# Recommender kernel: a fourth group transposed before the third's products, holds of the gathers moved, layers of the first 256 samples moved into tile 2, last tile in five groups

## What is computed

```python
h = relu(dense @ dw1 + db1)
dense_emb = relu(h @ dw2 + db2)                       # 512 x 64
sparse_emb = emb_tables[f_ids, sparse_idx]            # 512 x 26 x 64
emb = concat([dense_emb[:, None, :], sparse_emb], 1)  # 512 x 27 x 64
inter = einsum('bfd,bgd->bfg', emb, emb)
pairs = inter[:, iu0, iu1]                            # 351 per sample
z = concat([emb.reshape(512, -1), pairs], 1)
z = relu(z @ ow1 + ob1)                               # to 512
z = relu(z @ ow2 + ob2)                               # to 256
z = relu(z @ ow3 + ob3)                               # to 128
return z @ ow4 + ob4
```

## Time and profile before

| | us |
|---|---|
| median of 3 runs | 188.17 (187.83 to 189.74) |
| the profiled execution, its own time | 187.21 |
| its span | 185.4 |
| PE busy / POOL busy in the span | 127.4 / 123.8 |
| DVE busy / ACT busy | 37.8 / 42.2 |

### The profile page before, as it was taken

How to read it: one execution, slowest core, us unless ns; L and a number is a source line. 1 busy time by engine, 2 the same in 40 slices (tenths; PEclk the granted TensorE clock), 3 DMA queues, 4 the chain that set the end, 5 groups by cost and what they waited for, 6 DMA issues and landing times.

```text
span 185.4 us, 3069 instructions
## 1 busy us (share of the span) xinstructions
PE 127.4 (69%) x1301; PEld 68.8 (37%) x1301; DVE 37.8 (20%) x97; ACT 42.2 (23%) x96; POOL 123.8 (67%) x199
## 2 busy tenths in 40 slices
PE   1510285828655995839439993959729979989994
PEld 0000132514344442524226432424426446656453
DVE  2700003000142204100144005000234023136011
ACT  0440310031046201040075001040174011166011
POOL 3888888888735888888565888888367887200000
PEclk9999999975965699996965798587997999999999
DMA  5999532221212332312312332222222324100000
GB/s 157 409 332 357 172 26 23 23 28 21 21 13 23 21 22 24 28 22 26 24 13 24 23 27 20 23 28 20 19 20 20 22 25 31 18 4 0 4 0 0
DMA packets 4576, 9.80 MB, mean 53 GB/s; under 512 B 2065, under 2 KB 2065, under 8 KB 3922
## 3 DMA queue, kind: packets, MB, share of 16 engines
q0 software_dynamic: 3328, 3.41, 21.3%
q1 hardware_dynamic: 1010, 5.30, 7.1%
q10 hardware_dynamic: 224, 0.89, 1.6%
HBM read 9.59 MB, written 0.00 MB: 52 GB/s over the span
## 4 chain that ended last, share of the span: by engine, by line
PE 45%; POOL 26%; issue 18%; ACT 5%; DMA 3%; DVE 2%
PE acc L259 20%; POOL gathered L211 20%; PE acc L292 10%; PE inter L276 7%; POOL pace L219 6%; PE acc L310 4%; DMA gathered<-tables,rows 2%; ACT emb L386 1%; ACT emb L387 1%; PE turned L240 1%; PE acc L301 1%; ACT pairs L392 1%; DMA idx_raw<-idx 1%; ACT z L399 1%; DVE emb L466 1%
## 5 line engine op out<-in xcount | busy, mean ns | idle before, releaser
L211 POOL DMA_INDIRECT gathered<-tables,rows x104 | 98.9, 951 | 34.6 <-issue 16.9
L259 PE MATMUL acc<-w,emb 128*128 128x512 f32 x104 | 65.7, 780 | 19.4 <-issue 12.3
L259 PEld LDWEIGHTS acc<-w,emb 128*128 128x128 f32 x104 | 31.3, 315 | 46.3 <-issue 36.9
L392 ACT ACTIVATE pairs<-inter 28x96 f32<-28x96 f32 (+1 forms) x64 | 15.7, 246 | 39.8 <-PE inter L276 39.1
L219 POOL MEMSET pace<- 128x192 uint8 x90 | 24.7, 274 | 0.1
L292 PE MATMUL acc<-w,pairs 128*128 128x512 f32 x56 | 24.7, 592 | 0.0
L182 DVE COPY pairs<-inter 28x96 f32<-28x96 f32 (+1 forms) x64 | 17.0, 266 | 26.5 <-PE inter L276 25.8
L276 PE MATMUL inter<-emb 64*28 64x28 f32 x1024 | 12.6, 204 | 13.8 <-DMA gathered<-tables,rows 10.1
L240 PE MATMUL turned<-small,gathered 128*128 128x128 f32 x52 | 10.1, 317 | 13.5 <-DMA gathered<-tables,rows 13.5
L386 ACT ACTIVATE emb<-turned 128x512 f32<-128x512 f32 x8 | 8.8, 1098 | 45.7 <-issue 28.6
L465 DVE COPY emb<-turned 128x512 f32<-128x512 f32 (+1 forms) x7 | 5.5, 784 | 64.1 <-issue 49.5
(11 more groups left out here) (47 smaller groups left out, 26.3 us busy)
## 6 DMA issues: line engine op xcount, KB each, us to landing
w<-w SPq DMA_DIRECT2D x5, 1024.0 KB, 8.7
gathered<-tables,rows POOLq DMA_INDIRECT x104, 3.4
small<-small_pack ACTq DMA_DIRECT2D x1, 706.5 KB, 6.0
dense_sb<-dense_pack ACTq DMA_DIRECT2D x1, 160.5 KB
idx_raw<-idx SPq DMA_DIRECT2D x1, 39.0 KB
idx_raw<-idx SPq DMA_DIRECT2D x1, 13.0 KB, 1.9
out<-y SPq DMA_DIRECT2D x1, 2.0 KB
```

What stands on the lines that cost most here:

```text
L211: pool.indirect_dma_start(out=gathered[:, t, s, :], out_offset=None, in_=tables, in_offset=bass.IndirectOffsetOnAxis(ap=rows[:, t, s:s + 1 ...
L259: nc.tensor.matmul(acc[t][:], emb[:, tile_of(t), place(2 * c)], w[:, c, :], start=(c == 0), stop=False)
L392: last = move(lambda dst, src: nc.scalar.activation(dst, src, ACT.Copy), t, k, (0, 1))
```

## The change

- In tiles 0 to 2, turn(t, 3) stands ahead of field_products(t, 2), and field_products(t, 3) comes behind interactions(t, 0).
- The holds are at s = 4 and s = 7, the fifth and eighth gather.
- In a tile's loop the order is now: interactions(t-1, 0), field_products(t-1, 3), interactions(t-1, 1), turn(t, 0), pair_product(t-1), field_products(t, 0), z1_to_features(t-1), turn(t, 1), and so on. ACT's order follows.
- The last layers go in three parts in place of two: samples 0 to 255 in tile 2, 256 to 383 in tile 3, 384 to 511 at the end.
- Tile 3 has five groups, of 4, 4, 2, 2 and 1 chunks; the last one is kept by ACT and DVE together, as the fourth was.
- Ahead of the last layers of the last part PE waits for the first two outputs.

```diff
+LAST_GROUPS = [(0, 4), (4, 8), (8, 10), (10, 12), (12, 13)]
-EARLY = LAST * P
+PARTS = [slice(0, 2 * P), slice(2 * P, 3 * P), slice(3 * P, B)]
-HOLDS = [7, 10]
+HOLDS = [4, 7]
+def groups(t):
+    return LAST_GROUPS if t == LAST else GROUPS
...
             def kept(t, g):
-                pe.wait_ge(kept_dve if g % 2 else kept_act, t * 2 + g // 2 + 1)
-                if t == LAST and g == NG - 1:
-                    pe.wait_ge(kept_act, t * 2 + 3)
+                if g % 2 or g == NG:
+                    pe.wait_ge(kept_dve, t * 2 + g // 2 + 1)
+                if g % 2 == 0:
+                    pe.wait_ge(kept_act, t * 2 + g // 2 + 1)
...
             for t in range(TILES):
                 if t:
                     interactions(t - 1, 0)
+                    field_products(t - 1, 3)
+                    interactions(t - 1, 1)
                 turn(t, 0)
                 if t:
-                    interactions(t - 1, 1)
+                    pair_product(t - 1)
                 field_products(t, 0)
                 if t:
-                    pair_product(t - 1)
                     z1_to_features(t - 1, at_once)
                 turn(t, 1)
-                if t < LAST:
+                if t == LAST:
+                    break
+                if t == LAST - 1:
+                    layer2(PARTS[0], 1, whole, (acc[0], acc[1]))
+                    field_products(t, 1, 0, 2)
+                    layer3(PARTS[0], 0, acc[3])
+                    field_products(t, 1, 2)
+                    layer4(PARTS[0], 0, acc[0])
+                else:
                     field_products(t, 1)
-                    turn(t, 2)
-                    field_products(t, 2)
-                    turn(t, 3)
-                    field_products(t, 3)
-
-            layer2(early, LAST - 1, [[(m, k) for m in range(2) for k in range(K1)]], (acc[0], acc[1]))
-            c0, c1 = GROUPS[1]
-            field_products(LAST, 1, (c0, c0 + 1))
-            layer3(early, 0, acc[2])
-            field_products(LAST, 1, (c0 + 1, c0 + 3))
+                turn(t, 2)
+                turn(t, 3)
+                field_products(t, 2)
+
+            layer2(PARTS[1], 2, whole, (acc[1], acc[2]))
+            field_products(LAST, 1, 0, 2)
+            layer3(PARTS[1], 1, acc[1])
             turn(LAST, 2)
-            layer4(early, 0, acc[0])
-            field_products(LAST, 1, (c0 + 3, c1))
+            field_products(LAST, 1, 2)
+            layer4(PARTS[1], 1, acc[2])
+            field_products(LAST, 2)
             turn(LAST, 3)
-            c0, c1 = GROUPS[2]
+            field_products(LAST, 3, 0, 1)
+            turn(LAST, 4)
             interactions(LAST, 0)
-            field_products(LAST, 2, (c0, c0 + 2))
+            field_products(LAST, 3, 1)
+            field_products(LAST, 4)
             interactions(LAST, 1)
-            field_products(LAST, 2, (c0 + 2, c1))
-            field_products(LAST, 3)
             pair_product(LAST)
             z1_to_features(LAST, Z1_STEPS)
-            layer2(late, LAST, LAYER2_STEPS, (acc[1], acc[2]))
-            layer3(late, 1, turned[1])
-            layer4(late, 1, inter[0])
+            pe.wait_ge(y_done, 2)
+            layer2(PARTS[2], LAST, LAYER2_STEPS, (acc[1], acc[2]))
+            layer3(PARTS[2], 2, turned[1])
+            layer4(PARTS[2], 2, inter[0])
...
         (ACT's loop)
                 if t:
                     moves(t - 1, 0)
+                    moves(t - 1, 1)
                 keep(t, 0)
                 if t:
-                    moves(t - 1, 1)
                     z1_relu(t - 1, at_once)
+                if t == LAST - 1:
+                    z2_relu(PARTS[0], 0, acc[0])
+                    z3_relu(PARTS[0], 0, acc[3])
                 if t == LAST:
-                    z2_relu(early, 0, acc[0])
-                    z3_relu(early, 0, acc[2])
+                    z2_relu(PARTS[1], 1, acc[1])
+                    z3_relu(PARTS[1], 1, acc[1])
                 keep(t, 2)
...
         (DVE's loop)
                 keep(t, 1)
+                if t == LAST - 1:
+                    z2_relu(PARTS[0], 0, acc[1])
+                    outputs(PARTS[0], 0, acc[0])
                 if t == LAST:
-                    z2_relu(early, 0, acc[1])
-                    outputs(early, 0, acc[0])
-                if t < LAST:
-                    keep(t, 3)
+                    z2_relu(PARTS[1], 1, acc[2])
+                    outputs(PARTS[1], 1, acc[2])
+                keep(t, 3)
```

More of the change, by code:

```diff
@@ L124, in build @@
         ones_set = sem("ones_set")
-        group_in = [[sem(f"group_in{t}_{g}") for g in range(NG)] for t in range(TILES)]
+        group_in = [[sem(f"group_in{t}_{g}") for g in range(len(groups(t)))] for t in range(TILES)]
         gathers_held = sem("gathers_held")
@@ L257, in field_products @@
                 kept(t, g)
-                for c in range(*(chunks or GROUPS[g])):
+                c0, c1 = groups(t)[g]
+                for c in range(c0 + first, min(c0 + end, c1)):
                     nc.tensor.matmul(acc[t][:], emb[:, tile_of(t), place(2 * c)], w[:, c, :],
@@ L266, in interactions @@
                         pe.wait_ge(dense_placed, 1)
-                    kept(t, 2)
-                    kept(t, 3)
+                    for g in range(2, len(groups(t))):
+                        kept(t, g)
                     if t:
@@ L326, in layer4 @@
                 nc.tensor.matmul(bank[0:1, 0:n], ow4, z3t[:, samples], start=True, stop=True).then_inc(y_mm, 1)
[L328 removed]
             at_once = [(0, K1)]
+            whole = [[(m, k) for m in range(2) for k in range(K1)]]
             for t in range(TILES):
```

53 lines of the change are left out of this document (25 added, 28 removed).

## The result

The changed kernel takes 199.9 us (median of 4 runs, 198.09 to 200.84) where the kernel before takes 188.89 (4 runs, 187.83 to 189.74): ratio 1.0574 [1.0471, 1.0677], slower. The profiled execution took 200.32 us, with a span of 198.5 (before: 185.4). Every time in this document is the median over all executions of a kernel on its chip; the ratios leave out executions over 1.5% above the kernel's fastest, and where those left give no interval (e1, e3, e12) there is no ratio.

A forecast was written before the change was run, and what follows sets the result against it. Gathers and interactions in the holds bound it up to tile 3, then PE's work. Last gather 1.2 us later, moved layers 0, end 0.45 us earlier at 183.35; profiled 186.8 plus 0.96 gave 187.7 us (184.8 to 190.8).

The forecast's parts named there:

- Part 3: End, tile 3: removed layers paid back by later gathers and new waits; last pair product at 171.9, end at 183.35.
- Part 1: Holds of POOL's gathers: they cost 4.6 us a tile, 13.8 against 12.6 before; last gather 1.2 us later.
- T + 2.5 + 5.5 = T + 8.0: Earliest interactions after tile start T: third group's products begin 2.5 us in and take 5.5 us.
- The bound of plus 4: Holds: upper bound on the last gather's delay, plus 4 us, if all interactions take 2.95 us.
- Part 2: Tile 2: 5.1 us of moved layers fit a 2.44 us gap plus 2.6 us of regained clock; cost 0.
- the 7.0: End, tile 3: layers on 384 columns that leave the tile, summed as 5.4 + 0.8 + 0.8 us.
- (1): Rival, holds: third groups at full clock take 3.8 instead of 5.5 us; 3.2 less, 184.5; chance 0.29.
- (2): Rival, end: clock falls in new waits; 1.7 us more for the second, 3.2 for both, to 190.9; chance 0.17.
- The 3.4 us of the pair product: Rival about the end's clock: work-time of the last pair product going at half speed, 1.7 us more.
- (3): Rival, tile 2: PE misses the landing of s = 23; up to 2.6 us more, 190.2; chance 0.12.
- (4): Rival, end: moved layers weren't on the path, gathers' landing takes over; already in the sum, no chance of its own.

The follow-up runs named there:

- e1: The changed kernel with the old holds, at the eighth and eleventh gather, on chip B: 190.86 us (before there 184.44).
- e3: The changed kernel with four groups in tile 3 and the old order of its end, on chip B: 188.83 us (before there 184.44).
- e12: The changed kernel itself, run again on chip E: 196.54 us (before there 186.92).
- e4: The kernel before with only the last layers moved (256 samples in tile 2, 128 in tile 3), on chip B: 182.21 us, ratio 0.9888.
- e5: The changed kernel itself, run again on chip C: 186.72 us, ratio 1.0178.
- e8: The changed kernel with old holds and the last two chunks' products behind both last interactions, on chip C: 189.52 us, ratio 1.0289.
- e13: The e3 kernel (new holds, old end of tile 3), run again on chip E: 188.48 us, ratio 1.0066.
- e6: The changed kernel with old holds and old end of tile 3, keeping new order and moved layers, on chip C: 183.01 us, ratio 0.9942.
- e2: The changed kernel with the last layers of the first 384 samples back in tile 3 in one part, on chip B: 195.68 us, ratio 1.0498.
- e11: The e4 kernel (only the layers moved), run again on chip D: 182.72 us, ratio 0.9884.
- e9: The changed kernel with unused extra products filling PE's two new waits at the end, on chip D: 185.16 us, ratio 1.0048.
- e10: The changed kernel itself, run again on chip D: 186.71 us, ratio 1.0044.

## Why the prediction was wrong

The prediction, 187.7 (184.8 to 190.8), is 12 us below. Two of its own signs of being wrong came: the last gather began after 161 (161.63), and the clock was down in the last pair product (0.57). The step that failed most is in Part 3, where turn(3, 3) follows the products behind turn(3, 2) without a wait: 9.2 us lay between the starts of the two turns where 4.1 were forecast, and waits for late signals and the half clock behind them filled the difference. Its parts, in its own order:

**The holds (Part 1): the mechanism right, the price too low on chip A, and set against the wrong neighbour.** The turn ahead of the products cost nothing, interactions(0, 0) began at 48.39 (47.9 forecast) in one piece of 1.27 us, and the second holds were idle for 1.88 to 2.07 (near 2.1). The first holds were 3.60, 3.98 and 4.81 where 3.4 was forecast, and the last gather came 3.4 us later, not 1.2. The first ones exceed three times 3.4 by 2.2 us, which is the miss. The term that failed there is the 5.5 in "T + 2.5 + 5.5 = T + 8.0": the third group's products took 6.38 and 6.26 in tiles 0 and 1 (5.48 and 5.51 before), as more of them ran at half clock (mean granted clock 0.57 and 0.59 over them, before 0.67 and 0.68); in tile 2 the late keep put them back by 1.98. The bound of plus 4 held. On chips C and D the same products took 5.24 and 4.95 in tile 0, and the last gather came at 158.46 and 157.10, before the 159.4 forecast: there the sum was too high.

There is a second error in this term. It set the new holds against holds of 3.37 us and counted it as a gain that the gaps in the interactions vanish. On chip B, e4 runs before's code up to tile 2, with first holds of 1.69: where the gaps are missing, the old holds are cheaper by far. The new ones put the last gather 3.4 us and more later than the old ones (e5 against e8 on one chip; e3 and e13 against e6). A gain that consists in the vanishing of an unexplained gap was worth nothing on the chips that had no gap.

The Trainium skill (Runtime: NRT & Kernel Launch, Instruction fetch mechanics) holds the crossing of blocks of 256 instructions to be mostly hidden. In the change the first interactions of each tile, in one piece, agree with that; the gaps of 0.59, 0.52 (before), 1.78 (e2) and 1.45 us (e8) do not, if that is their cause. The traces leave it open. Each has ten loads of 16 KB on an instruction queue, which they do not tie to an engine. In e2 one runs from 169.96 to 171.00, and the gap opens at 170.47; in e8 one runs from 167.27 to 168.23, and the gap opens at 168.18. In no block of interactions without a gap does a load start before the last 0.25 us, so for these two gaps a load is the candidate. For those of before it is not: both of tile 0 are over at 52.39, ahead of the next load at 53.38.

**The layers in tile 2 (Part 2): right.** Layer2 took 3.72 us (3.7 forecast), no wait stood ahead of the products of group 1 and they ran at full clock (1.00 from 111 to 122.4). Cost 0 on the path was right, and e4 and e11 show more: the kernel gains 1.1% by this edit alone, and in e4's trace tile 3 reaches the last landing in time. The prediction netted this gain against later gathers and new waits without giving it a number, and so did not see that the other parts spend it.

**The end (Part 3): the term that failed.** "turn(3, 2) at 157, products to 161.1. turn(3, 3) then". It was 159.80 on chip A, and turn(3, 3) 168.98: 7.9 us late, of which 2.8 was there by turn(3, 2), some 4 is PE's waits for the late signals (2.43 and 1.25), and 1 half clock (3.10 for four products that took 1.99). No row of before that the prediction used shows such a wait; the nearest is the 0.75 us of its z3t, which was not looked for. turn(3, 4) came at 172.84 for 163.9 (8.9 late), and from there to the end of y it took 24.08 for the 19.45 forecast: 4.6 more. 8.9 and 4.6 are the 13.6 us by which the whole is off (196.92 for 183.35). A slip of Part 3 changed nothing: it counts layer3 on 384 columns once, at 0.8, where its two products took 1.46 us (158.43 to 159.89 in before's trace); the forecast's path does not use the 7.0 that it adds up with it.

The waits themselves were forecast well: 1.35 us ahead of group 3's first chunk (1.5) and 2.42 ahead of the last pair product (2.3), in every run with the new end. On e5's chip the forecast's path holds to about 2 us: turn(3, 4) at 162.17 for 163.9, pair product 170.31 for 171.9, end at 181.91 for 183.35. There the change is still slower than before, by 1.8%, because before is itself faster there by 4.6 us (184.32 for 188.89): where its interactions have no gaps, the gathers with its holds run 2.8 us ahead of chip A's (e4's 155.38 for 158.22); no trace of before from another chip is there, so the rest of the 4.6 is open. On chip D the ratio is 1.0044 [0.9993, 1.0096], and the forecast's own, 187.7 to 188.17, was 0.9975.

**The rivals.** (1), third groups at full clock: on chip A they went the other way, to 6.4 and 6.3 us in tiles 0 and 1. (2), the clock falls in the new waits of the end: it came, and its price from the last turn to the end is 4.3 us (24.08 against 19.74 in e5; 23.87 in e1; 22.71 in e12, where behind the last turn it fell in the pair product alone) where up to 3.2 was forecast. The 3.4 us of the pair product that it puts at half speed stand in no row: this product took 7.94 us, 1.8 more than at full clock, and 9.23 in e12, 3.1 more. The mechanism is right as far as this: with the wait ahead of group 3 open the clock fell behind it in e1 and e8, and with both waits filled it stayed at 1.00 in e9's trace. But it is no rule: the same waits stood in e5 and e10 at clock 1.00. And on chip A the clock was already down when the 1.35 us came; it fell behind the waits for the late signals. (3), PE late in tile 2: layer2 was in time, but keep(2, 2) was 2.6 us late for another reason, and the price went the way described there, into the hold (4.81). (4), the landing takes over: so it was in e4 and e5; on chip A it was not, PE came 7.8 us behind the landing.

**What stays open.** Why PE's signals reach the other engines up to 5.2 us late on two of the five chips. All cases lie around the layers woven between products and turns while POOL gathers; with the old end they were smaller (0.75 us before on chip A, up to 2.0 in e13). The traces of these two chips alone lack records, and whether the lateness would be there without the recording is not known. e1 and e2 ran on a chip where nothing was late, so whether the cutting of the layers matters was not tried where it counts. That e12 is slower than e13 is shown, by 8.1 us of their medians; the split into lateness and clock is not.

## What to carry to other kernels

Price each part of a combined change against the best neighbour and not only against the kernel before: here one part gained 1.1% by itself, and the others lost it again and more, by amounts that do not add up (e5, e6 and e8). When an order at the end of a kernel is changed, write down what stood behind each hand-over: six MATMULs moved ahead of the last turn left 1.35 and 2.42 us uncovered, and a wait that is cheap in itself costs 3 to 4 us more in the executions in which PE's clock falls behind it. Before an odd wait is explained, compare how complete the traces are. And let no gain rest on a gap that isn't explained, or on one chip.

## What the runs showed of the hardware that was not expected

- The rise of a semaphore by TensorE reached ScalarE and VectorE up to 5.2 us behind the end of the matmul in the trace, on two chips of five, around layer2 to layer4; elsewhere a step took 0.03 to 0.11 us. The cause is open. The four traces of these two chips lack 19 to 26 of some 140 rises and a quarter to over a third of the landings of DMAs, the other eleven hardly any.
- The changed kernel took 186.7 us on two chips, 196.5 on another and 199.9 on a fourth, where the kernel before took 184.3 and 185.0, 186.9 and 188.9: its spread is nearly three times as wide.
- The granted clock fell from 1.00 to 0.50 behind waits of 1.35 us and of 2.4 to 3.1 us in some executions, and stayed at 1.00 behind the same 1.35 and 2.42 in others (e5, e10). When it fell, the stretch from the last turn to the end took 3.0 to 4.3 us more (e12, e1 and the change against e5).
- Gaps with no releaser, 0.5 to 1.8 us, stand within a run of interactions in some traces and at other places of it in others, or nowhere. Two of them (1.78 us in e2, 1.45 in e8) open 0.5 and 0.9 us behind the start of a 16 KB load of instructions; those of before have no such load.
